# Local attention blocks: the softmax weights divided before the value product, the product written feature-major, the output transposes gone

## What is computed

```python
sim = jnp.einsum('bhwie,bhwje->bhwij', bq, bk2) * QK_SCALE    # a window of queries against its own and the previous window
sim = jnp.where(mask, -jnp.finfo(sim.dtype).max, sim)
attn = jax.nn.softmax(sim, -1)
out = jnp.einsum('bhwij,bhwje->bhwie', attn, bv2)
out = out.transpose(0, 2, 1, 3).reshape(b, n, INNER)
return out @ Wo
```

## Time and profile before

| | |
|---|---|
| runs | 5030.15 us median of 3 (5025.54 to 5031.53) |
| profiled execution | span 5028.6 us; its time beside the span is not listed apart |
| instructions | 220082 |
| PE busy | 4506.2 us (90%) |
| DVE busy | 3884.2 us (77%) |
| ACT busy | 3169.0 us (63%) |
| POOL busy | 2725.1 us (54%) |

### The profile page before, as it was taken

How to read it: one execution, slowest core, us unless ns; L and a number is a source line. 1 busy time by engine, 2 the same in 40 slices (tenths; PEclk the granted TensorE clock), 3 DMA queues, 4 the chain that set the end, 5 groups by cost and what they waited for, 6 DMA issues and landing times. The chain is left out here.

```text
span 5028.6 us, 220082 instructions
## 1 busy us (share of the span) xinstructions
PE 4506.2 (90%) x82384; PEld 3378.9 (67%) x82384; DVE 3884.2 (77%) x8191; ACT 3169.0 (63%) x6718; POOL 2725.1 (54%) x3917
## 2 busy tenths in 40 slices
PE   3568949999999999999999999999998687999996
PEld 3556726777777777777777777777776454666665
DVE  6985567888888888888888888888886766777775
ACT  2004526777777777777777777777776445777775
POOL 0012136666666666766666766666664335555552
PEclk7988969999999999999999999999999688999998
DMA  2001134555555555555555555555553004444442
GB/s 78 1 1 33 40 85 124 145 139 143 140 145 138 139 142 137 143 134 151 135 149 132 151 137 146 135 147 136 147 136 97 11 13 110 116 111 117 116 113 76
DMA packets 704922, 564.46 MB, mean 112 GB/s; under 512 B 223492, under 2 KB 629864, under 8 KB 704008
## 3 DMA queue, kind: packets, MB, share of 16 engines
q1 hardware_dynamic: 691080, 537.36, 40.4%
q10 hardware_dynamic: 13312, 22.02, 1.4%
HBM read 359.38 MB, written 200.02 MB: 111 GB/s over the span
## 5 line engine op out<-in xcount | busy, mean ns | idle before, releaser
L2156 POOL TENSOR_TENSOR L_qk<-L_cos_part,L_sin_part 128x512 f32<-128x512 f32 x896 | 1128.3, 1273 | 98.1 <-DVE L_sin_part L2033 96.3
L1817 ACT ACTIVATE L_squares<-L_ps_q 128x512 f32<-128x512 f32 x896 | 534.9, 597 | 818.0 <-PE L_ps_q L1543 811.7
L1543 PE MATMUL L_ps_q<-L_w_qkv,L_xT 128*128 128x512 f32 x1792 | 980.0, 629 | 13.6 <-DVE L_sin_part L2033 10.3
L2147 POOL TENSOR_TENSOR L_qk<-L_qk,L_rnorm 128x1024 f32<-128x1024 f32 (+1 forms) x512 | 864.2, 1688 | 17.8 <-POOL L_rnorm L2130 0.5
L1579 PEld LDWEIGHTS L_ps_t<-L_ident,L_qk 128*128 128x128 f32 x3584 | 447.0, 141 | 479.5 <-issue 380.0
L2032 DVE TENSOR_TENSOR L_cos_part<-L_ps_q,L_rot 128x512 f32<-128x512 f32 x896 | 610.9, 682 | 38.9 <-POOL L_rot L2166 30.9
L2033 DVE TENSOR_TENSOR L_sin_part<-L_ps_q,L_rot 128x512 f32<-128x512 f32 x896 | 610.9, 682 | 0.0
L2034 DVE TENSOR_REDUCE L_sumsq<-L_squares 128x8 f32<-128x512 f32 x896 | 606.7, 677 | 0.0
L2124 POOL TENSOR_TENSOR L_nw_a<-L_rnorm 128x32 f32<-128x32 f32 (+1 forms) x256 | 59.5, 232 | 907.1 <-ACT L_rnorm L1847 907.0
L1579 PE MATMUL L_ps_t<-L_ident,L_qk 128*128 128x128 f32 x3584 | 540.3, 273 | 5.3 <-POOL L_qk L2147 2.7
L1828 ACT ACTIVATE L_qkT<-L_ps_t 128x512 f32<-128x512 f32 x896 | 530.6, 592 | 15.5 <-PE L_ps_t L1579 15.5
(11 more groups left out here) (294 smaller groups left out, 8851.0 us busy)
## 6 DMA issues: line engine op xcount, KB each, us to landing
L_val<-v_rows SPq DMA_DIRECT2D x896, 260.0 KB, 3.9
v_rows<-L_val SPq DMA_DIRECT2D x384, 260.0 KB, 2.1
v_rows<-L_val SPq DMA_DIRECT2D x512, 65.0 KB, 2.0
L_rot_base<-in_rot SPq DMA_DIRECT2D x256, 128.0 KB
v_rows<-L_val SPq DMA_DIRECT2D x128, 130.0 KB, 2.1
L_x_in<-x_rows SPq DMA_DIRECT2D x512, 32.0 KB, 1.7
mid_rows<-z SPq DMA_DIRECT2D x256, 64.0 KB, 1.6
L_f_in<-mid_rows SPq DMA_DIRECT2D x256, 64.0 KB, 2.0
```

What stands on the lines that cost most here:

```text
L1543: nc.tensor.matmul(ps_q[j % 2][:, :], xT[:, parity(t), :], w_qkv[:, 0:2, 256 * j:256 * j + 256], start=True, stop=True).then_inc(S["proj_p ...
L1817: nc.scalar.activation(squares[:, j % 2, :], ps_q[j % 2][:, :], ACT.Square).then_inc(S["sq_done"], 1)
L2147: nc.gpsimd.tensor_tensor(v, v, r, ALU.mult).then_inc(S["normed"], 1)
L2156: nc.gpsimd.tensor_tensor(qk[:, t % 2, h, s, :], cos_part[:, j % 2, :], sin_part[:, j % 2, :], ALU.add).then_inc(S["added"], 1)
```

## The change

The probabilities are divided by their row sums before they are transposed, and the value product is turned round, so that its result has features on partitions, which is the layout that the output product wants.

- DVE `normalise` is gone. A new `row_sums` stands in its place at the head of DVE's half: a sum over the probabilities (128x512, from SBUF) after the exponentials of the half before, and a reciprocal of 8 columns (L0) or 4 (L1).
- A new `weigh` on POOL multiplies the probabilities by the reciprocals (128x512, in place). It is first in POOL's half. The probability transposes wait for it (`weighted`) where they waited for the exponentials.
- The weighted values have the values as the stationary operand (64 rows by 64 columns in L0, 128 by 64 in L1) and the probabilities as the moving one (32 columns in L0, 64 in L1). Their number stays the same, and the order is now queries, window, row half, column half.
- `out_transposes` is gone, with its waits. `out_copy` on ACT copies straight from the product's banks and waits for the product.
- The column of ones is gone, so a row of stored values has 512 elements (was 520) in L0 and 256 (was 260) in L1.
- In L0 the output weights are loaded by four DMAs into a changed row order (was one).
- The up projections and the scores wait for `out_copy` where they waited for `normalise`.

```diff
-                        wait(dve, S["att_done"], halves(k, t, h - 1))
-                        dve.wait_ge(S["pv_ps"], halves(k, t, h))
-                        sums = p_rec[:, :].rearrange("x (p u) -> x p u", p=2)
-                        nc.vector.reciprocal(sums, O_VIEW[:, :, :, 64]).then_inc(S["rec_done"], 1)
...
-                        nc.vector.tensor_tensor(dst, O_VIEW[:, :, :, 0:64], rec, ALU.mult).then_inc(S["att_done"], 1)
+                def row_sums(k, T, hf):
+                    t, h = item(T, hf, AT_PV)
+                    if live(k, t):
+                        wait(dve, S["rec_done"], halves(k, t, h - 1))
+                        dve.wait_ge(S["exp_done"], halves(k, t, h))
+                        nc.vector.tensor_reduce(p_sum[:, :], probs[:, h, :].rearrange("x (n k) -> x n k", n=2 * HU), AX.X, ALU.add).then_inc(S["sum_done"], 1)
+                        wait(dve, S["weighted"], halves(k, t, h - 1))
+                        dve.wait_ge(S["sum_done"], halves(k, t, h))
+                        nc.vector.reciprocal(p_rec[:, :], p_sum[:, :]).then_inc(S["rec_done"], 1)
...
+                def weigh(k, T, hf):
+                    t, h = item(T, hf, AT_PV)
+                    if live(k, t):
+                        pool.wait_ge(S["rec_done"], halves(k, t, h))
+                        pr = probs[:, h, :].rearrange("x (n k) -> x n k", n=2 * HU)
+                        rec = p_rec[:, :].rearrange("x (n o) -> x n o", o=1).to_broadcast([128, 2 * HU, 2 * W])
+                        nc.gpsimd.tensor_tensor(pr, pr, rec, ALU.mult).then_inc(S["weighted"], 1)
...
-                        pe.wait_ge(S["exp_done"], halves(k, t, h))
+                        pe.wait_ge(S["weighted"], halves(k, t, h))
...
-                        for i in range(HU):
+                        for ii in range(2):
                             for a in range(NB):
-                                for p in range(2):
-                                    out = O_VIEW[W * a:W * a + W, p, i, :]
-                                    if NB == 4:
-                                        rows = slice(64 * p, 64 * p + 64)
-                                        last = nc.tensor.matmul(out, probsT[rows, i, W * a:W * a + W], val2[rows, tp, h, a, i, :], start=True, stop=True)
+                                queries = slice(128 * ii + W * a, 128 * ii + W * a + W)
+                                for p in range(NS):
+                                    for j in range(2):
+                                        out = ps_o[64 * j:64 * j + 64, p, queries]
+                                        if NB == 4:
+                                            rows, i = slice(64 * p, 64 * p + 64), 2 * ii + j
+                                            last = nc.tensor.matmul(out, val2[rows, tp, h, a, i, :], probsT[rows, i, W * a:W * a + W], start=True, stop=True)
...
-                            wait(pe, S["att_done"], halves(k, T - 5, 0))
+                            wait(pe, S["oT_done"], halves(k, T - 5, 0))
...
-                    out_transposes(k, T, hf)
...
-                        act.wait_ge(S["oT_ps"], halves(k, t, h))
+                        act.wait_ge(S["pv_ps"], halves(k, t, h))
```

More of the change, by code:

```diff
@@ L1241, in local_block_stage @@
         CONSTS = 16 * 6
-        ZEROED = 8
+        ZEROED = 7
+        WO_LOADS = 4 if NB == 4 else 1
         HEAD_START = 128
@@ L1351, in windows @@
         def windows(par, h, at):
-            rows = v_rows[par, h, :, at:at + 260]
-            return bass.AP(rows.tensor, rows.offset, [[ROW, 2 * W], [W * ROW, NB], [1, 260]])
+            rows = v_rows[par, h, :, at:at + 256]
+            return bass.AP(rows.tensor, rows.offset, [[ROW, 2 * W], [W * ROW, NB], [1, 256]])
         with nc.Block() as block:
@@ L1400, in load_output_weights @@
                     l = layer_of(k, 0)
-                    sp.dma_start(w_out[:, :, :], W_["out"][l, :, :].rearrange("(u p) n -> p u n", p=128)).then_inc(S["wo_in"], 16)
+                    if NB == 4:
+                        src = W_["out"][l, :, :].rearrange("(g j p d) n -> j p d g n", j=2, p=2, d=64)
+                        for j in range(2):
+                            for p in range(2):
+                                sp.dma_start(w_out[64 * j:64 * j + 64, :, :].rearrange("d (p g) n -> d p g n", p=2)[:, p, :, :], src[j, p]).then_inc(S["wo_in"], 16)
+                    else:
+                        sp.dma_start(w_out[:, :, :], W_["out"][l, :, :].rearrange("(u p) n -> p u n", p=128)).then_inc(S["wo_in"], 16)
                 def load_up(k):
@@ L1555, in value_bank_read @@
                         wait(pe, S["val_done"], halves(k, T - 3, hf))
-                        if not live(k, T - 3):
-                            wait(pe, S["oT_done"], halves(k, T - 5, hf))
                     else:
@@ L1606, in values @@
                         if NS == 2:
-                            wait(pe, S["oT_done"], halves(k, t - 2, h))
                             wait(pe, S["val_done"], halves(k, t, h - 1))
@@ L1635, in output @@
                     if live(k, t):
-                        pe.wait_ge(S["wo_in"], reloads(k, t, 16))
+                        pe.wait_ge(S["wo_in"], reloads(k, t, 16 * WO_LOADS))
+                        if NS == 2 and not live(k, item(T, 1, AT_PROJ)[0]) and parity(T) == TO_FT % 2:
+                            wait(pe, S["new_done"], groups_(k, T - TO_DOWN))
                         wait(pe, S["rotated"], steps_(k, T - 2, 2 * NS - 2))
@@ L1661, in scores @@
                             pe.wait_ge(S["pT_done"], halves(k, v, g))
-                            wait(pe, S["att_done"], halves(k, v, g - 1))
+                            wait(pe, S["oT_done"], halves(k, v, g - 1))
                         else:
@@ L1726, in up_projections @@
                             elif made == "up_ps":
-                                t, h = item(T, 0, AT_OUT)
-                                wait(pe, S["oT_done"], halves(k, t, h))
+                                wait(pe, S["hidden_done"], groups_(k, t0 - 2))
                             for j, c in which:
@@ L2099, in emit @@
                 def emit(k, T, hf):
-                    normalise(k, T, hf)
+                    row_sums(k, T, hf)
                     shift(k, T, hf)
@@ L2189, in emit @@
                 def emit(k, T, hf):
+                    weigh(k, T, hf)
                     if hf == 0:
@@ L2209, in two_layer_kernel @@
     qkv = [dram(f"l0_{n}", [4096, w]) for n, w in (("q", 128), ("k", 128), ("v", 144))]
-    v_rows = [dram(f"v_rows{l}", [2, 2, w + 128, n]) for l, w, n in ((0, 32, 520), (1, 64, 260))]
+    v_rows = [dram(f"v_rows{l}", [2, 2, w + 128, n]) for l, w, n in ((0, 32, 512), (1, 64, 256))]
     x_rows, mid_rows = dram("x_rows", [ROWS, 128]), dram("mid_rows", [ROWS, 128])
```

57 lines of the change are left out of this document (18 added, 39 removed).

## The result

The changed kernel takes 5079.8 us (median of 4 runs, 5076.7 to 5081.1), the kernel before 5029.4 us beside it: ratio 1.0096, 95% interval 1.0084 to 1.0109. It is slower by 50 us, where 16 us more had been forecast, on the same side and inside the range. The profiled execution spans 5074.8 us (before 5028.6).

What follows compares the result with a forecast made beforehand. TensorE's stream was taken to bound L0 (busy 3021 of 3065 us). L0 +20 and L1 -6 made +14, with the pipelines' ends +16: span 5044.6, median 5046 us, slower by 0.3%; range 4968 to 5100.

Steps and rivals of the forecast that it cites:

- Transposes: L0, TensorE: without the output transposes the second q/k transposes start earlier, gaining 0.34 us in halves A, C and D.
- Product turned round: L0's weighted values: change of tile form and slower pace cost 0.40 us in halves B, C, D and 0.34 in A.
- Rivals 1 and 2: L0's value product gets no dearer, 4926 us, chance 0.12; or its change of form is hidden, about 4990 us, chance 0.20.
- Half A: L0's half A: 0.34 us gained from the removed transposes and 0.34 us lost on the value product, 0.00 in sum.
- The waits of the output transposes: L0, TensorE: 33.0 us of waits for DVE's multiply go, 14 already counted and about 5 returning, so -14 us.
- Half B: L0's half B: 0.17 us gained, as DVE's row sums wait for exponentials, against 0.40 for the product: +0.23 us.
- some 0.15 of such a wait in each B is in the B I counted from: L0: 14 us of the removed waits for DVE's multiply were taken as already inside the half B used for counting.
- L1: L1: removed transposes bring nothing, alternating column halves about 0.05 us a half, so -6 us in 128 halves.
- some 0.3 us more a half, covered by its 207 idle us: DVE in L1: takes some 0.3 us more a half, which its 207 idle us of 784 were to cover.
- POOL: POOL's new multiply: 1.04 us each, load in L0 from 67% to 80%, done 1.0 us before the probability transposes in B.
- Rival 3: The chain over DVE and POOL comes late for TensorE's probability transposes, 96 us more, 5142 us; chance 0.08.
- The ends: Filling and emptying of the two pipelines: a longer chain adds a few us, taking the total from +14 to +16.

Runs made afterwards that it cites:

- e3: Changed kernel with four 128x128 transposes with no reader put back in L0 where the output's transposes were; 5145.0 us, ratio 1.0233.
- e4: Changed kernel with 32 weighted-values matmuls of 64 moving columns in L0 in place of 64, every second window's values left out; 4939.7 us, ratio 0.9828.
- e8: Changed kernel with each weighted-values matmul of 64 features in L0 made as two of 32, in 64x32 tiles as the scores; 6513.3 us, ratio 1.2947.
- e1: Changed kernel with DVE taking the maximum ahead of the row sums and the shift behind them, in both stages; 5057.2 us, ratio 1.0060.
- e10: Changed kernel without the row sums, the reciprocal taken of a constant, so outputs are not normalised; 5019.1 us, ratio 0.9981.
- e11: Changed kernel with maximum first and, in halves B, C, D, value projection before second q/k transposes in L0; L1 from the kernel before; 5011.7 us, ratio 0.997.
- e2: Changed kernel with DVE's row sums and reciprocal behind both instructions of the shift; 5182.1 us, ratio 1.031.
- e12: Changed kernel with one more POOL multiply of the same shape, into a buffer with no reader, ahead of `weigh` in every half; 5218.5 us, ratio 1.0372.

## Why the prediction was right, and where its sizes were off

The direction and its cause were right: the product turned round costs more than the transposes give. But 46 us on the spans stand against 16, and the misses partly cancel.

- **Transposes, 0.34 us in a plain half: right in C and D, wrong in A.** C and D gained 0.33 and 0.34, and e3 gives the same by itself. The second transposes were said to start at 2.35 us and do at 2.30. In A only 0.12 us came through, because the weighted values there wait for the gated rows. The forecast had no such wait in A.
- **Product turned round, +0.40: right in kind, 0.04 short.** The pace of 14.4 ns was met (14.5, and 15.4 in e4 with twice the columns), the end of 0.15 too. The change of form was mis-sized: I took 0.17 us, the weight loads' idle of the earlier trace rows, counted from nothing; it is 0.21, because before the product had started 0.06 us ahead of the last score. That is 12 us over B, C and D. Rivals 1 and 2 fall with it; e4 and e8 show both prices apart.
- **Half A, 0.00: wrong by 0.14 to 0.16 us, 13 to 15 us in all.** The forecast had -0.34 + 0.34. Measured is -0.12 + 0.28: the gain was capped, the step of form is hidden behind the wait, and the old group took 0.78 us in the median, where I had read 0.89 from one half.
- **The waits of the output transposes, -14 us: right to 3 us.** Of the 33.0 us, 14.7 lay in the halves B, 12.5 in A at the loop turns and the rest in the first rounds. The loop turns gave about 11 us back, and this is what holds A's mean at +0.01.
- **Half B, +0.23: two errors that partly cancel, which is luck.** B was worked out from one half of 8.12 us; only 3 of 87 are that short, and the mean is 8.31. The term "some 0.15 of such a wait in each B is in the B I counted from" was false: the halves have it (0.17 us in the mean), that one had none. So the old B was 0.19 us too short. The new B was forecast at 8.35 and came to 8.62, 0.27 too short. The rotation was forecast at 3.0 us and starts at 3.01 in the half shown, at 3.12 in the median; the output product was forecast at 4.43 us and comes at 4.53 and 4.63. Together +0.31 in place of +0.23, 8 us. e1 and e10 show that this is DVE's chain behind the exponentials.
- **L1, -6 us: wrong sign.** The up projections do wait for `out_copy` (2.65 us in place of 2.05), and A pays nothing, as forecast: its length stays 7.32. The product group gave the forecast 0.05 us in each half (0.62 in place of 0.67 in B, C and D), of which C and D kept 0.05 and 0.02. But "some 0.3 us more a half, covered by its 207 idle us" is the step that failed: DVE's idle share covers nothing where the sums stand in its queue ahead of the shift for which TensorE's next transposes wait. +0.35 in B, +9 us over the stage; e10 takes it away, e11 avoids it.
- **POOL: right.** 1.04 us, 79% where 80% was forecast, cover of 0.95 to 1.6 us in L0 where 1.0 was. Rival 3 did not come; e2 and e12 show how near it was.
- **The ends: wrong sign.** The chain at the emptying of L0 got shorter by 9 us, where a few us for a longer one had been added.

Together: +50 in L0 where +20 stood, +9 in L1 where -6 stood, -13 for the ends where +2 stood: 46 against 16 on the spans. The miss of 34 us on the median is as large as the two widths named in the prediction together (20 and 15 us); without the ends, which went the other way by luck, it would have been 15 us more.

## What to carry to other kernels

Count small matmuls by their weight loads and by changes of tile form before you count moved columns: the change of form between scores and product cost 0.21 us a half here, and the pace 0.23. When a reduction moves from a result to its inputs, ask in which strict queue it now stands and who waits for what is behind it; a queue's order was worth as much (0.41 us in B) as leaving the reduction out. Follow each kind of half to its own last wait: a gain of 0.34 us in front of a wait for another engine was worth 0.12. And take the length of a half from all its occurrences: one clean half hid 0.2 us of waits, and a mean that did not move hid 0.14 us of loss.

## What the runs showed of the hardware

- One 64-row weight load with its fp32 matmul costs 14.5 ns with 64 columns loaded and 32 moved, 15.4 with 64 moved (e4), 10.8 with 32 loaded and 65 moved (kernel before), 9.5 with 32 loaded and 32 moved (e8, its stops left out). With 32 moved, half the columns loaded thus cost two thirds, not half. The Trainium skill, "TensorE: Matmul & The Clock Gate", section "LDWEIGHTS (loading the stationary operand)", has columns/1.2 ns, which makes an estimate of 13.3 ns for the first with four tiles side by side; the trace is 1.2 above it.
- Two groups of the same form, 64x32 tiles, overlap: the next one starts 0.06 us before the last matmul of the group ahead (kernel before, e8). With 64x64 tiles behind 64x32 it starts 0.15 us after it. L1 changes form in both kernels (64x64 to 128x64), and there it is 0.20 us in both.
- On DVE, a 128x512 instruction that needs the one ahead starts 0.79 us behind that one's start (shift behind maximum), one that does not 0.61 (sums behind maximum in e1); medians over more than 300 pairs each.
- 192 small matmuls in a row stop TensorE, for 2.0 us in the median, with no semaphore behind it (e8). 128 do not in the loop, but do in the straight code at the ends of L0. The reason is open.
